# Group norm and softmax attention over 16 images: GpSimd's last wait before the doubled chunk dropped, exact exponentials through PSUM, image 0 rearranged

## The reference

```python
xg = group_norm(x, 32 groups)                 # no scale or shift
q, k, v = split(xg @ W_qkv)                   # 256 channels each, n = 4096 positions
k = softmax(k over the n positions)
context = k^T @ v                             # 256 x 256
out = x + (q @ context) @ W_out + b_out
```

## Time and profile before

| | |
|---|---|
| median of 3 runs | 1231.55 us (1230.2 to 1232.49) |
| profiled execution | 1231.76 us, its span 1230.0 us |
| PE busy | 1197.5 us, 97% of the span |
| DVE busy | 893.0 us, 73% |
| ACT busy | 838.9 us, 68% |
| POOL busy | 639.1 us, 52% |
| DMA | 216 GB/s from and to HBM over the span |
| granted PE clock, mean | 0.997 |

### The profile page before, as it was taken

The page is one execution under the profiler, slowest core; times in us unless marked ns, Lnnn a source line. Parts: engine busy times, 40 slices in busy tenths (PEclk is TensorE's granted clock), DMA queues, the critical chain, the costliest instruction groups (busy, mean ns, idle before and its releaser), DMA issues.

```text
span 1230.0 us, 21431 instructions
## 1 busy us (share of the span) xinstructions
PE 1197.5 (97%) x8460; PEld 1119.3 (91%) x8460; DVE 893.0 (73%) x1585; ACT 838.9 (68%) x1140; POOL 639.1 (52%) x285
## 2 busy tenths in 40 slices
PE   4799999999999999999999999999999999999998
PEld 4798999989999998999989999998989989999897
DVE  6887767777677777768777677777767778677561
ACT  5576767676685776757676686776847767576754
POOL 7365563634646365563644636356453654536520
PEclk9999999999999999999999999999999999999999
DMA  8348666586765758666486665767657586573524
GB/s 330 115 155 308 222 218 227 178 287 206 248 210 194 270 176 289 224 202 240 163 296 224 228 208 195 267 205 274 202 176 261 184 285 223 183 253 121 187 77 163
DMA packets 107062, 266.71 MB, mean 217 GB/s; under 512 B 10193, under 2 KB 10193, under 8 KB 106961
## 3 DMA queue, kind: packets, MB, share of 16 engines
q1 hardware_dynamic: 106960, 265.33, 62.8%
HBM read 198.18 MB, written 67.11 MB: 216 GB/s over the span
## 4 chain that ended last, share of the span: by engine, by line
PE 91%; DVE 6%; ACT 1%; DMA 1%; issue 0%; SPq 0%; DVEq 0%; ACTq 0%
PE ps_k L362 28%; PE ps_e L522 19%; PE ps_e L531 10%; PE ps_g L450 5%; PE ps_g L441 5%; PE ps_g L443 5%; PE ps_e L450 4%; PE ps_e L441 4%; PE ps_e L443 4%; DVE e_lo L865 3%; PE ps_g L469 1%; PE ps_g L486 1%; DVE e_raw L859 1%; PE ps_g L500 1%; PE ps_g L492 1%; DVE bn L784 1%
## 5 line engine op out<-in xcount | busy, mean ns | idle before, releaser
L315 POOL TENSOR_TENSOR xt_lo<-xt_raw,xt_hi 128x1024 fp32r<-128x1024 f32 x128 | 307.3, 2403 | 457.0 <-ACT xt_hi L625 330.1
L321 POOL TENSOR_TENSOR x_lo<-x_raw,x_hi 128x1024 fp32r<-128x1024 f32 x128 | 304.9, 2398 | 44.5 <-ACT x_hi L630 44.2
L834 DVE TENSOR_TENSOR mx<-ps_k,mx 128x256 f32<-128x256 f32 x480 | 203.1, 423 | 97.2 <-ACT e_raw L634 76.3
L677 ACT ACTIVATE o_stage<-ps_e,bias 128x512 f32<-128x512 f32 x253 | 170.6, 688 | 117.5 <-PE ps_e L531 117.5
L865 DVE TENSOR_TENSOR e_lo<-e_raw,e_hi 128x1024 fp32r<-128x1024 f32 x128 | 204.4, 1599 | 19.7 <-ACT e_raw L643 19.5
L362 PE MATMUL ps_k<-wk_hi,xt_hi 128*128 128x256 f32 x1024 | 206.3, 283 | 0.0
L362 PE MATMUL ps_k<-wk_lo,xt_hi 128*128 128x256 f32 x1024 | 205.2, 282 | 0.0
L634 ACT ACTIVATE e_raw<-ps_k 128x512 f32<-128x512 f32 x256 | 141.2, 594 | 89.1 <-PE ps_k L362 88.8
L791 DVE BATCH_NORM_STATS2 bn<-xs 128x6 f32<-128x512 f32 x240 | 154.3, 686 | 39.9 <-DMA xs<-in_xt_dram 39.0
L642 ACT ACTIVATE e_hi<-e_raw 128x1024 fp32r<-128x1024 f32 x128 | 135.1, 1055 | 69.0 <-DVE e_raw L859 36.4
L362 PEld LDWEIGHTS ps_k<-wk_hi,xt_hi 128*128 128x128 f32 x1024 | 162.8, 189 | 7.0
(11 more groups left out here) (120 smaller groups left out, 1958.7 us busy)
## 6 DMA issues: line engine op xcount, KB each, us to landing
xt_raw<-in_xt_dram SPq DMA_DIRECT2D x128, 512.0 KB, 4.3
x_raw<-in_xn_dram SPq DMA_DIRECT2D x128, 512.0 KB, 3.4
out_dram<-o_stage SPq DMA_DIRECT2D x128, 512.0 KB, 4.6
xs<-in_xt_dram SPq DMA_DIRECT2D x240, 256.0 KB, 5.1
w_setup<-in_w_dram SPq DMA_DIRECT2D x2, 256.0 KB, 9.9
wk<-in_w_dram SPq DMA_DIRECT2D x1, 256.0 KB, 10.0
wq_t<-in_w_dram SPq DMA_DIRECT2D x1, 256.0 KB, 11.3
b_col<-in_b_out_dram SPq DMA_DIRECT2D x1, 1.0 KB, 10.4
```

What stands on the lines that cost most here:

```text
L315: nc.gpsimd.tensor_tensor(xt_lo[:, s], xt_raw[:, s], xt_hi[:, s].bitcast(F32), ALU.subtract).then_inc(xt_lo_ready, 1)
L321: nc.gpsimd.tensor_tensor(x_lo[:, s], x_raw[:, s], x_hi[:, s, :, 0:C].bitcast(F32), ALU.subtract).then_inc(x_lo_ready, 1)
L677: nc.scalar.activation(o_stage[:, u % O_SLOTS, h, :], src, ACT.Identity, bias=bias[:, h:h + 1]).then_inc(o_ready, 1)
L834: nc.vector.tensor_tensor(mx[:], tile, mx[:], ALU.max).then_inc(max_done, 1)
```

## The change

GpSimd's wait for `u_lo_ready` before xt_low 2 is deleted. In the upper half of each image (chunks 4 to 7) the exact exponentials go to the two PSUM banks `ps_k[:, 1]` in place of `e_raw`, and `e_low` reads them there; since that is one buffer, ACT waits before chunks 5 to 7 until the `e_low` before has read it, and before chunk 4 until the variance has left these banks. For image 1's statistics other columns are used. In image 0, GpSimd makes the low parts of the exponentials of chunks 0 to 2, four of DVE's bn halves and the sum behind them move into the gather, and the mean, the variance and rstd of image 1 come later.

```diff
--- before.py
+++ after.py
@@ -26,6 +26,7 @@
 XS_AFTER = {0: (4, 8), 2: (8, 12), 3: (12, 16)}
 
 FIRST_XT = (8, 11, 15)
+POOL_LOW = 3
 
 
 def build(nc: bass.Bass, xt: bass.AP, xn: bass.AP, w: bass.AP, b_out: bass.AP, out: bass.AP):
@@ -129,6 +130,8 @@
         ps_g0 = psum("ps_g0", [P, CB, CH])
         ps_e = psum("ps_e", [P, CB, CH])
         ps_g = (ps_g0, ps_e)
+
+        ps_exp = ps_k[:, 1].rearrange("p h n -> p (h n)")
 
         wk_loaded = sem("wk_loaded")
         wvo_loaded = sem("wvo_loaded")
@@ -167,6 +170,7 @@
         alpha_ready = sem("alpha_ready")
         sub_done = sem("sub_done")
         e_ready = sem("e_ready")
+        e_lo_first = sem("e_lo_first")
         e_hi_ready = sem("e_hi_ready")
         e_lo_ready = sem("e_lo_ready")
         g_ps = sem("g_ps")
@@ -201,6 +205,14 @@
             for b in range(B):
                 period(b, b % 2, b < B - 1, b < B - 2)
 
+        def e_lo_count(b, j):
+
+            return b * NCH + j + 1 - POOL_LOW
+
+        def stats_psum(b, which):
+
+            return ps_k[:, 0, 0, C + which * CB:C + (which + 1) * CB] if b == 1 else ps_k[:, 1, which, 0:CB]
+
         def combined(b):
 
             return (u_sb, m_hi, m_lo) if b < B - 1 else (u_last, wk_hi, wk_lo)
@@ -321,6 +333,11 @@
                 nc.gpsimd.tensor_tensor(x_lo[:, s], x_raw[:, s], x_hi[:, s, :, 0:C].bitcast(F32),
                                         ALU.subtract).then_inc(x_lo_ready, 1)
 
+            def first_e_low(j):
+                pool.wait_ge(e_ready, j + 1)
+                nc.gpsimd.tensor_tensor(e_lo[:, j], e_raw[:, j], e_hi[:, j % E_SLOTS].bitcast(F32),
+                                        ALU.subtract).then_inc(e_lo_first, 1)
+
             def rstd_of(b, parity):
                 pool.wait_ge(var_eps_ready, b + 1)
                 nc.gpsimd.tensor_tensor(rstd[:, parity], var_eps[:], neg_half[:], ALU.pow).then_inc(rstd_ready, 1)
@@ -335,18 +352,22 @@
                 x_low(0, j)
             pool.wait_ge(setup_sb, 3)
             nc.gpsimd.tensor_tensor(wq_lo[:], wq_t[:], wq_hi[:].bitcast(F32), ALU.subtract).then_inc(wq_lo_ready, 1)
+            for j in range(POOL_LOW):
+                first_e_low(j)
 
             def period(b, parity, more, more2):
                 n, np_ = b + 1, 1 - parity
                 if more:
                     xt_low(n, np_, 0)
-                    rstd_of(n, np_)
+                    if b:
+                        rstd_of(n, np_)
                 for j in range(HALF, NCH):
                     x_low(b, j)
+                    if b == 0 and j == NCH - 2:
+                        rstd_of(n, np_)
                 if more:
                     pool.wait_ge(wk_ready, n + 1)
                     xt_low(n, np_, 1)
-                    pool.wait_ge(u_lo_ready, b * CB + CB)
                     xt_low(n, np_, 2)
                     for j in range(X_SLOTS):
                         x_low(n, j)
@@ -422,11 +443,11 @@
 
             def stats_mean(b):
                 pe.wait_ge(mv_ready, b + 1)
-                nc.tensor.matmul(ps_k[:, 1, 0, 0:CB], grp[:], mv[:, :, 0], start=True, stop=True).then_inc(mean_ps, 1)
+                nc.tensor.matmul(stats_psum(b, 0), grp[:], mv[:, :, 0], start=True, stop=True).then_inc(mean_ps, 1)
 
             def stats_var(b):
                 pe.wait_ge(var2_ready, b + 1)
-                nc.tensor.matmul(ps_k[:, 1, 1, 0:CB], grp[:], var2[:], start=True, stop=True).then_inc(var_ps, 1)
+                nc.tensor.matmul(stats_psum(b, 1), grp[:], var2[:], start=True, stop=True).then_inc(var_ps, 1)
 
             def gather_high(b, j):
                 pe.wait_ge(e_hi_ready, b * NCH + (j + 1))
@@ -444,7 +465,10 @@
                                          start=False, stop=False, skip_group_check=True)
 
             def gather_low(b, j):
-                pe.wait_ge(e_lo_ready, b * NCH + (j + 1))
+                if b == 0 and j < POOL_LOW:
+                    pe.wait_ge(e_lo_first, j + 1)
+                else:
+                    pe.wait_ge(e_lo_ready, e_lo_count(b, j))
                 for t in range(TILES):
                     for d in range(CB):
                         last = nc.tensor.matmul(ps_g[j // HALF][:, d, 0:C + 2], e_lo[:, j, t, d * P:(d + 1) * P],
@@ -571,16 +595,20 @@
                 n, np_ = b + 1, 1 - parity
                 gather_high(b, 0)
                 turn_max(b, 1)
-                if more:
+                if more and b:
                     stats_mean(n)
                 gather_low(b, 0)
                 gather_high(b, 1)
                 spread_max(b, 1)
-                if more:
+                if more and b:
                     stats_var(n)
                 gather_low(b, 1)
                 for j in range(2, NCH):
                     gather(b, j)
+                    if b == 0 and j == 3:
+                        stats_mean(n)
+                    if b == 0 and j == 4:
+                        stats_var(n)
 
                 if more:
                     keys_tiles(n, np_, 0, 0, 4)
@@ -640,7 +668,12 @@
                 if j >= E_SLOTS:
                     act.wait_ge(g_ps, b * NCH + (j - E_SLOTS + 1))
                 nc.scalar.activation(e_hi[:, j % E_SLOTS], e_raw[:, j], ACT.Exp).then_inc(e_hi_ready, 1)
-                nc.scalar.activation(e_raw[:, j], e_raw[:, j], ACT.Exp).then_inc(e_ready, 1)
+                if j > HALF:
+                    act.wait_ge(e_lo_ready, e_lo_count(b, j - 1))
+                if j == HALF and 0 < b < B - 1:
+                    act.wait_ge(var_eps_ready, b + 2)
+                to = ps_exp if j >= HALF else e_raw[:, j].rearrange("p t c -> p (t c)")
+                nc.scalar.activation(to, e_raw[:, j].rearrange("p t c -> p (t c)"), ACT.Exp).then_inc(e_ready, 1)
 
             def scales(b):
                 act.wait_ge(dm_ready, b + 1)
@@ -799,8 +832,8 @@
 
             def mean_of(b, parity):
                 dve.wait_ge(mean_ps, b + 1)
-                nc.vector.tensor_tensor(dev[:], mv[:, :, 0], ps_k[:, 1, 0, 0:CB], ALU.subtract)
-                nc.vector.tensor_scalar(neg_mean[:, parity, :], ps_k[:, 1, 0, 0:CB], -1.0, None,
+                nc.vector.tensor_tensor(dev[:], mv[:, :, 0], stats_psum(b, 0), ALU.subtract)
+                nc.vector.tensor_scalar(neg_mean[:, parity, :], stats_psum(b, 0), -1.0, None,
                                         ALU.mult).then_inc(mean_read, 1)
                 dve.wait_ge(mean_read, b + 1)
                 for c in range(CB):
@@ -810,7 +843,7 @@
 
             def var_of(b):
                 dve.wait_ge(var_ps, b + 1)
-                nc.vector.tensor_scalar(var_eps[:], ps_k[:, 1, 1, 0:CB], EPS, None, ALU.add).then_inc(var_eps_ready, 1)
+                nc.vector.tensor_scalar(var_eps[:], stats_psum(b, 1), EPS, None, ALU.add).then_inc(var_eps_ready, 1)
 
             def wk_low(b, parity):
                 dve.wait_ge(wk_hi_ready, b + 1)
@@ -862,7 +895,9 @@
 
             def e_low(b, j):
                 dve.wait_ge(e_ready, b * NCH + (j + 1))
-                nc.vector.tensor_tensor(e_lo[:, j], e_raw[:, j], e_hi[:, j % E_SLOTS].bitcast(F32),
+                exact = ps_exp if j >= HALF else e_raw[:, j].rearrange("p t c -> p (t c)")
+                nc.vector.tensor_tensor(e_lo[:, j].rearrange("p t c -> p (t c)"), exact,
+                                        e_hi[:, j % E_SLOTS].bitcast(F32).rearrange("p t c -> p (t c)"),
                                         ALU.subtract).then_inc(e_lo_ready, 1)
 
             def take_first(b):
@@ -955,33 +990,44 @@
                                     ALU.subtract).then_inc(wvo_lo_ready, 1)
             for j in range(HALF):
                 key_maxes(0, j)
-                for q in range(4 + 2 * j, 6 + 2 * j if j < HALF - 1 else 11):
+                for q in ((4, 5), (6, 7), (8,), ())[j]:
                     bn_half(1, q)
             block_max(0, 0)
-            for q in range(11, 14):
+            for q in range(9, 12):
                 bn_half(1, q)
             key_maxes(0, 4)
-            bn_half(1, 14)
             shift(0, 0)
             key_maxes(0, 5)
             shift(0, 1)
-            bn_half(1, 15)
             shift(0, 2)
             key_maxes(0, 6)
-            e_low(0, 0)
             shift(0, 3)
-            bn_sum(1)
             key_maxes(0, 7)
-            e_low(0, 1)
-
-            def period(b, parity, more, more2):
+
+            def first_gather():
+                block_max(0, 1)
+                block_scales(0)
+                mean_bias(0, 0)
+                bn_half(1, 12)
+                bn_half(1, 13)
+                shift(0, 4)
+                e_low(0, 3)
+                bn_half(1, 14)
+                bn_half(1, 15)
+                bn_sum(1)
+                shift(0, 5)
+                e_low(0, 4)
+                mean_of(1, 1)
+                take_first(0)
+                shift(0, 6)
+                var_of(1)
+                e_low(0, 5)
+                shift(0, 7)
+                e_low(0, 6)
+                e_low(0, 7)
+
```

(22 more changed lines are left out.)

## The result

The changed kernel takes 1239.91 us (median of 4 runs, 1237.88 to 1241.84) against 1231.55, which is 8.4 us more. The ratio, taken over the fast runs of both kernels, is 1.0073, 95% interval 1.0055 to 1.009. It is slower, as forecast, but by 8.4 us and not by 18.9. The profiled execution is the fastest of the four, 1237.88 us with a span of 1236.0, so the traces differ by 6.0.

A forecast was written before the change was run, and what follows sets the result against it. The prediction took PE's own work as the floor, leaving only its idle time and clock to change. From 1231.76 us, -4.5 -3.2 -3.1 +18.9 +10.8 = +18.9 gave 1250.7, stated as 1250; range 1217 to 1264.

The forecast's parts named there:

- stalls of e_low gone: Chunks 4 to 7: e_low reading PSUM is not kept out by POOL, so five stalls of 0.9 go, 4.5 us.
- image 0: Image 0's new order: earlier gather and less lateness gain 5.7, a later stall pays back 2.5; net -3.2 us.
- image 11's stall: Image 11's existing 3.1 us loss from a late m_low, subtracted because it is one of the fifteen forecast stalls.
- m_low kept out: Without the wait, x_low 2 starts before m_low in every image; PE stalls 1.26 in 15 images, +18.9 us.
- clock behind it: PE's granted clock falls after the m_low stall in somewhat under half the images: 0.7 each, +10.8 us.
- The step on the deleted wait: Early xt_low 2 delays acc_low at no PE cost; x_low 2 then beats m_low, +18.9 us before clock loss.
- The reading that a lead of 0.04 decides: When POOL and DVE contend, whichever starts first keeps the other out; a lead of 0.04 us is enough.
- rival (B): DVE's m_low issues first and no image stalls: 1221 or 1218 us, from a POOL spacing of 2.24; chance 0.27.
- PE's floor: In a quiet image PE is busy for all of 74.10 us, so only its idle time and clock can change.
- The PSUM part's cost on ACT: ACT's new wait before exact exponentials is free in an undisturbed image: e_low 6 is issued 1.9 us early enough.
- The pay-back of 2.5: In image 0, late xt_low 2 holds acc_low, x_low 0 precedes its second half, and PE waits: +2.5 us.
- rival (D): xt_low 2 comes late in every image; second acc_low loses to x_low 0, PE stalls 2.5: 1275 us, chance 0.05.

The follow-up runs named there:

- the delays: Changed kernel plus an unread GpSimd memset before x_low 2, in three sizes: 128x2 1239.77 us, 128x96 1216.46 us, 128x160 1215.35 us.
- the middle delay: Changed kernel plus an unread 128x96 memset on GpSimd before x_low 2: 1216.46 us, a single run.
- the larger delays: Changed kernel plus an unread GpSimd memset of 128x96 or 128x160 before x_low 2: 1216.46 us and 1215.35 us.
- the largest delay: Changed kernel plus an unread 128x160 memset on GpSimd before x_low 2: 1215.35 us, ratio 0.9884, four runs.
- the smallest delay: Changed kernel plus an unread 128x2 memset on GpSimd before x_low 2: 1239.77 us, a single run.
- POOL's wait for m_low: Changed kernel plus a GpSimd wait for m_low before x_low 2, xt_low 2 staying early: 1216.95 us, ratio 0.9894.

## Why the prediction was right or wrong

The direction and the cause were right, and the size was wrong by more than half. By its terms, on the spans of the profiled executions:

| Term | Predicted | Measured | From |
|---|---|---|---|
| stalls of e_low gone | -4.5 | -8.0 | 1045.24 and 70.89 against 1035.08 and 69.82, less 3.2 for image 11 |
| image 0 | -3.2 (-5.7 and +2.5) | -3.8 (-4.3 and +0.5) | 79.04 to 74.78; its product stage against the others |
| image 11's stall | -3.1 | -3.2 | 77.14 against 73.93 |
| m_low kept out | +18.9 | +19.1 | 15 x (75.20 - 73.93) |
| clock behind it | +10.8 | +1.5 | one image at 76.75 of fourteen |
| sum | +18.9 | +5.6, and 6.0 between the spans | |

The step on the deleted wait held in nearly each point: acc_low kept out and done by T+3.3 at no cost in most images, x_low 2 at T+8.68 forecast and 8.70 found, m_low behind it by 0.09 forecast and 0.07 found, the stall 1.26 and 1.27, in all fifteen images. The reading that a lead of 0.04 decides is what carried it, and the delays bear it out from both sides. It was a narrow matter: the middle delay moves the two starts against each other by 0.1, as much as rival (B) asked for, and turns the result. Rival (B) had its mechanism right: it is the kernel with the larger delays, and the point from which it decides is the lead of 0.07 that the trace shows.

The step that failed is the clock: "under half of the images, 0.7 each". It was sized from one stall, image 11's, after which the clock fell: 1.56 late by the operand, 1.40 between matmuls in rows 6. (And 15 times 0.7 is 10.5; the sum has 10.8.) The stalls here are 1.14 between matmuls, and the clock fell once in the profiled run, in the image that took 76.75; the other three runs, 2 to 4 us longer at a mean clock of 0.997 against 0.999, fit one or two falls more, which no trace shows. In the kernel with only the wait deleted it fell behind eleven of the twelve stalls of 1.93, and behind two of the four of 1.1. One case was no basis: with PSUM alone image 11 had the same stall of 1.4, and the clock stayed up. The longer stalls cost the clock more often, but these kernels differ in more than the length, and what makes one short stall of many bring it down stays open. With this term at 1.5 the forecast's sum is 1241.4. The execution that the 1.5 is read from took 1237.9, and the 3.5 between them is the PSUM part, below. That the forecast's time without any clock loss, 1240, is the median measured is luck: the two errors, a few falls and the larger gain, cancel.

The gain of the PSUM part was forecast too small by 3.5, since I took the quiet image of rows 1 (74.10) for PE's floor. It still held 0.2 of e_low's lateness, in waits too short to stand out, and the last image 1.1 rather than 0.9. That PE's busy time filled the stretch did not mean that it ran as fast as it could. Some 3 us before the end of its gather, where PE comes from e_low's matmuls, two matmuls start 0.23 and 0.19 behind the ones before, where 0.12 is usual. That is the 0.2, and no gap shows, because a record there is longer (0.36 against 0.28). In the kernel with the wait back neither delay is there, and with image 0's order alone both are. A slip in the reading of rows 3 changes nothing: the 2.08 counts from POOL's start, and DVE waited 2.04. The PSUM part's cost on ACT was rightly put at nothing, with one wait of 0.6 in image 0. Its write to PSUM takes 1.01, in SBUF 1.05.

In image 0 the start of the gather moved to 50.27 and not to 48.7: the first keys ended at 34.01 and not at 32.72. In all eight kernels with this order the gather starts 16.2 to 16.3 behind that end, which lies between 32.66 and 34.10, so the 1.3 is not the change's doing. The first eight matmuls of both kernels, before and after:

```profile
21.11 1.34 PE L362 MATMUL ps_k<-wk_hi,xt_hi 128*128 128x256 f32 x8
```

```profile
21.12 2.27 PE L383 MATMUL ps_k<-wk_hi,xt_hi 128*128 128x256 f32 x8
```

The granted clock reads 1.00 in both, so why they were slower here is not shown. With the wait back, the same order ended image 0's gather at 73.95, with the largest delay at 73.40, close to the 73.3 that the prediction's step gives. The pay-back of 2.5 came out as 0.5: xt_low 2 started at T+0.76 and not at T+1.0, so the second half of acc_low was just ahead of x_low 0. In the kernel with only the wait deleted it started at T+1.0 in twelve images, and acc_low was done at T+6.03 as the prediction has it for image 0; that was rival (D), with the right place and the wrong kernel.

The Trainium skill's rule (SBUF — State Buffer, Who interferes with whom) held as far as these runs go: e_low with one input in PSUM was never kept out, 64 of 64 between 1.209 and 1.227, although 47 of them start inside one of POOL's subtractions (16 more than 0.5 us before its end), and m_low with both inputs in SBUF was whenever it came second.

## What to carry to other kernels

When DVE and POOL both read two tensors from SBUF, the one that starts first delays the other by up to nearly its whole length (2.0 of 2.2 us here), so a short step of DVE's critical chain must not start just behind a long one of POOL's: compare the starts to 0.05 us, not only the busy shares. A wait that seems to hold an engine back for nothing (POOL had 330 us to spare) may be what keeps its next step out of the way; ask which step it lets through before it goes, and if it must go, protect the critical one directly or fill the consumer's gap. And a gain measured in the same change can hide it: with the wait back this change is worth 1.1%, without it it costs 0.7%.

## What the runs showed of the hardware

- Leads of 0.02 to 0.05 us decide who is kept out, in all images: POOL first by 0.02 to 0.05, m_low 2.69 to 2.73; DVE first by 0.03 to 0.04, m_low 0.692 in all fifteen.
- With POOL wholly out of the way m_low is 0.69; with the old wait it is 0.78 to 0.80: xt_low 2 (2.41 from T+6.60 in rows 5) is still under way when it starts at T+8.77. That 0.1 is not what makes an image 73.84 to 73.85 with the larger delays against 73.93, since with POOL's wait for m_low it is 0.69 too and the image 73.93; where that 0.09 comes from is open.
- POOL's memset, which only writes, does not keep m_low out: the 128x96 write from 231.71 to 231.90 overlaps m_low's start at 231.82, and m_low takes 0.69.
- The granted clock fell behind 5 of 34 stalls of 1.1 us (1 of 15 in the changed kernel, 2 of 15 with the smallest delay, 2 of 4 with only the wait deleted), behind 1 of 2 of 1.4 (image 11 before, and its like with PSUM alone), and behind 11 of 12 stalls of 1.9.
